# Swapping the rotated query halves by SBUF to SBUF transfers in an attention and FFN kernel

## The reference, cut to what matters

```python
q_nope = (q_c @ W_q_nope).reshape(Bx, Tx, H, NOPE_D)
q_rope = (q_c @ W_q_rope).reshape(Bx, Tx, H, ROPE_D)      # ROPE_D = 64
# rope: x * cos + rotate_half(x) * sin,  rotate_half(x) = concat(-x[32:], x[:32])
q = jnp.concatenate([q_nope, _apply_rope(q_rope, cos, sin)], axis=-1)
attn = softmax(causal(q @ k.T * scale));  out = attn @ v
```

## Time and profile before

| | |
|---|---|
| median of 3 runs | 709.99 us (708.76 to 710.64) |
| span of the profiled execution | 704.9 us |
| difference of the median to that span | 5.1 us |
| busy: TensorE, VectorE, ScalarE, GpSimd | 88%, 76%, 65%, 68% of the span |
| granted TensorE clock, mean | 0.951 |

### The profile page before, as it was taken

How to read it: one execution, slowest core, us unless ns; L and a number is a source line. 1 busy time by engine, 2 the same in 40 slices (tenths; PEclk the granted TensorE clock), 3 DMA queues, 4 the chain that set the end, 5 groups by cost and what they waited for, 6 DMA issues and landing times.

```text
span 704.9 us, 15757 instructions
## 1 busy us (share of the span) xinstructions
PE 622.8 (88%) x6279; PEld 486.1 (69%) x6282; DVE 534.4 (76%) x822; ACT 460.4 (65%) x715; POOL 477.0 (68%) x256
## 2 busy tenths in 40 slices
PE   7989888768989989998998998999899989985956
PEld 5666566557867678776876786778678867774635
DVE  6734889965667968786877777878778777875896
ACT  3465755666766757675768767767687677764754
POOL 2478499955577687768877777877797878710226
PEclk9687999999999999999999999999999999997979
DMA  9773975688898998999989998999799879796003
GB/s 260 255 236 125 225 153 95 109 156 169 206 165 150 159 166 162 147 163 186 181 137 157 156 149 150 165 178 168 131 165 157 151 132 162 134 153 106 9 1 119
DMA packets 323607, 108.32 MB, mean 154 GB/s; under 512 B 305808, under 2 KB 314576, under 8 KB 323408
## 3 DMA queue, kind: packets, MB, share of 16 engines
q1 hardware_dynamic: 322752, 106.74, 79.6%
q10 hardware_dynamic: 784, 0.59, 0.3%
HBM read 21.30 MB, written 10.49 MB: 45 GB/s over the span
## 4 chain that ended last, share of the span: by engine, by line
PE 40%; DVE 27%; ACT 11%; issue 10%; DMA 6%; POOL 5%; SPq 1%; POOLq 0%; DVEq 0%; ACTq 0%
PE psum L1066 37%; DVE small L869 10%; DVE p_src L877 6%; ACT psum L685 5%; DMA pt<-p_src 4%; ACT p_src L679 2%; DMA acc<-in_L_attn_x 2%; DVE o_lo L901 2%; DVE hid L1046 1%; ACT o_hi L667 1%; DVE small L1015 1%; POOL res L540 1%; DVE acc L768 1%; DVE acc L907 1%; PE psum L1267 1%
## 5 line engine op out<-in xcount | busy, mean ns | idle before, releaser
L679 ACT ACTIVATE p_src<-psum,small 128x1024 f16<-128x1024 f32 (+7 forms) x256 | 183.3, 742 | 177.9 <-DVE small L869 177.8
L869 DVE TENSOR_REDUCE small<-psum 128x1 f32<-128x1024 f32 (+7 forms) x256 | 186.3, 748 | 35.0 <-PE psum L1066 34.6
L877 DVE TENSOR_TENSOR p_src<-psum,p_src 128x1024 f16<-128x1024 f32 (+2 forms) x192 | 182.3, 949 | 33.0 <-ACT psum L685 32.5
L685 ACT ACTIVATE psum<-psum,small 128x1024 f32<-128x1024 f32 (+7 forms) x256 | 178.0, 718 | 0.0
L1066 PE MATMUL psum<-k_hi,q_hi 128*128 128x512 f32 (+2 forms) x384 | 159.2, 415 | 20.5 <-DVE p_src L877 10.1
L1066 PE MATMUL psum<-kv_tok,pt 128*128 128x65 f16 (+1 forms) x3456 | 144.3, 197 | 30.6 <-DVE p_src L877 16.7
L1066 PEld LDWEIGHTS psum<-kv_tok,pt 128*128 128x128 f16 x3456 | 121.4, 99 | 71.0 <-issue 35.3
L473 POOL TENSOR_TENSOR q_swap<-q_raw,sin_sb 32x1024 f32<-32x1024 f32 x32 | 75.8, 2370 | 97.7 <-ACT q_raw L613 97.1
L1066 PE MATMUL psum<-k_hi,q_lo 128*128 128x512 f32 (+2 forms) x384 | 133.8, 348 | 0.0
L1066 PE MATMUL psum<-k_lo,q_hi 128*128 128x512 f32 (+2 forms) x384 | 133.3, 347 | 0.0
L1066 PEld LDWEIGHTS psum<-k_hi,q_hi 128*128 128x128 f32 x384 | 75.6, 197 | 29.3 <-issue 12.7
(11 more groups left out here) (160 smaller groups left out, 924.4 us busy)
## 6 DMA issues: line engine op xcount, KB each, us to landing
pt<-p_src SPq DMA_TRANSPOSE x288, 3.5
wq_split<-w_split SPq DMA_DIRECT2D x4, 1024.0 KB, 5.0
k_rotated<-k_split SPq DMA_DIRECT2D x8, 512.0 KB, 3.4
wq<-wq_split SPq DMA_DIRECT2D x16, 256.0 KB, 4.0
acc<-in_L_attn_x SPq DMA_DIRECT2D x4, 512.0 KB, 7.7
ffn_t<-in_L_attn_W_o SPq DMA_DIRECT2D x1, 2048.0 KB, 19.4
k_hi<-k_rotated SPq DMA_DIRECT2D x8, 256.0 KB, 4.4
k_lo<-k_rotated SPq DMA_DIRECT2D x8, 256.0 KB, 4.9
```

The source lines that it names most:

```text
L679: ins = act.activation(p_src[u][:, 0, at:at + w], psum[:, COLS[i]:COLS[i] + w], ACT.Exp, bias=nb)
L685: ins = act.activation(ps, ps, ACT.Exp, bias=nb)
L869: dve.tensor_reduce(sm["mcol"][:, NT * (n % 2) + i:NT * (n % 2) + i + 1], psum[:, COLS[i]:COLS[i] + (i + 1) * P], AX.X, ALU.max, negate=True)\
L877: dve.tensor_tensor(p_src[u][:, 1, :], psum[:, o:o + WIDE[u]], p_src[u][:, 0, :], ALU.subtract)\
```

## The change

Three edits go together. The second GpSimd product goes away: SP copies the two halves of the raw query, swapped, from `q_raw` to `q_swap` by two SBUF to SBUF transfers of 32 partitions and 4 KB each (128 KB per transfer), and POOL multiplies all 64 partitions by the sine table in one instruction and subtracts instead of adding. POOL's wait for the copy of chunk 1 becomes a wait for these transfers, and SP takes over the wait for that copy and one for the previous head's rotation, which frees `q_swap`. SP issues the transfers ahead of the turning of unit 4 (in step 1: of unit 5), those of heads 0 and 1 ahead of the last weight stores of the prologue. And unit 1, which has 512 keys, joins `ONCE`: its two halves go in one turning transfer.

```diff
-ONCE = (3, 4, 5)
+ONCE = (1, 3, 4, 5)
...
+            def swap_halves(m, *chunks):
+                for idx in chunks:
+                    sp.wait_ge(misc_used(idx), USERS_AHEAD[idx] + 1)
+                if m:
+                    sp.wait_ge(S["pool_step"], 3 * m)
+                hr = ROPE // 2
+                for a in range(2):
+                    sp.dma_start(q_swap[a * hr:(a + 1) * hr, :], q_raw[m % 2][(1 - a) * hr:(2 - a) * hr, :])\
+                      .then_inc(S["swap_in"], 16)
...
             for r in range(2):
                 load_wq(r, r)
+            swap_halves(0, 0, 1)
+            swap_halves(1, 2, 3)
             store_wq(2)
             store_wq(3)
...
+                        if n + 2 < LAST and u == (5 if n == 1 else 4):
+                            swap_halves(n + 2, misc_index(n, "query", 0), misc_index(n, "query", 1))
                         turn_unit(n, u)
...
-            def rotate(n, idx):
+            def rotate(n):
                 raw = q_raw[n % 2]
-                pool.wait_ge(misc_used(idx), USERS_AHEAD[idx] + 1)
-                pool.tensor_tensor(q_swap[0:HR, :], raw[HR:ROPE, :], sin_sb[HR:ROPE, :], ALU.mult)\
-                    .then_inc(S["pool_step"], 1)
-                pool.wait_ge(S["pool_step"], 4 * n + 1)
-                pool.tensor_tensor(q_swap[HR:ROPE, :], raw[0:HR, :], sin_sb[0:HR, :], ALU.mult)\
-                    .then_inc(S["pool_step"], 1)
-                pool.wait_ge(S["pool_step"], 4 * n + 2)
+                pool.wait_ge(S["swap_in"], 32 * (n + 1))
+                pool.tensor_tensor(q_swap[:, :], q_swap[:, :], sin_sb[0:ROPE, :], ALU.mult).then_inc(S["pool_step"], 1)
                 pool.tensor_tensor(raw[0:ROPE, :], raw[0:ROPE, :], cos_sb[0:ROPE, :], ALU.mult)\
                     .then_inc(S["pool_step"], 1)
-                pool.wait_ge(S["pool_step"], 4 * n + 3)
-                pool.tensor_tensor(raw[0:ROPE, :], raw[0:ROPE, :], q_swap[:, :], ALU.add).then_inc(S["pool_step"], 1)
-                pool.wait_ge(S["pool_step"], 4 * n + 4)
+                pool.wait_ge(S["pool_step"], 3 * n + 2)
+                pool.tensor_tensor(raw[0:ROPE, :], raw[0:ROPE, :], q_swap[:, :], ALU.subtract).then_inc(S["pool_step"], 1)
+                pool.wait_ge(S["pool_step"], 3 * n + 3)
```

More of the change, by code:

```diff
@@ L256, in build @@
             score_done max_done hi_done exp_done lo_done pv_done rest_done head_read misc_full misc6_used misc7_used
-            pool_step qhi_done qlo_done o_hi_done norm_step
+            swap_in pool_step qhi_done qlo_done o_hi_done norm_step
             att_pool att_sp f_quant_dve
@@ L466, in _ @@
             weight_low(1)
-            HR = ROPE // 2
-            def rotate(n, idx):
+            def rotate(n):
                 raw = q_raw[n % 2]
-                pool.wait_ge(misc_used(idx), USERS_AHEAD[idx] + 1)
-                pool.tensor_tensor(q_swap[0:HR, :], raw[HR:ROPE, :], sin_sb[HR:ROPE, :], ALU.mult)\
-                    .then_inc(S["pool_step"], 1)
-                pool.wait_ge(S["pool_step"], 4 * n + 1)
-                pool.tensor_tensor(q_swap[HR:ROPE, :], raw[0:HR, :], sin_sb[0:HR, :], ALU.mult)\
-                    .then_inc(S["pool_step"], 1)
-                pool.wait_ge(S["pool_step"], 4 * n + 2)
+                pool.wait_ge(S["swap_in"], 32 * (n + 1))
+                pool.tensor_tensor(q_swap[:, :], q_swap[:, :], sin_sb[0:ROPE, :], ALU.mult).then_inc(S["pool_step"], 1)
                 pool.tensor_tensor(raw[0:ROPE, :], raw[0:ROPE, :], cos_sb[0:ROPE, :], ALU.mult)\
                     .then_inc(S["pool_step"], 1)
-                pool.wait_ge(S["pool_step"], 4 * n + 3)
-                pool.tensor_tensor(raw[0:ROPE, :], raw[0:ROPE, :], q_swap[:, :], ALU.add).then_inc(S["pool_step"], 1)
-                pool.wait_ge(S["pool_step"], 4 * n + 4)
+                pool.wait_ge(S["pool_step"], 3 * n + 2)
+                pool.tensor_tensor(raw[0:ROPE, :], raw[0:ROPE, :], q_swap[:, :], ALU.subtract).then_inc(S["pool_step"], 1)
+                pool.wait_ge(S["pool_step"], 3 * n + 3)
             def split_query(n):
@@ L496, in _ @@
             pool.wait_ge(S["wqr_lo"], 2 * 2)
-            rotate(0, 1)
+            rotate(0)
             pool.wait_ge(S["down_psum"], 2 * NPART)
@@ L516, in _ @@
                 if n + 1 < LAST:
-                    rotate(n + 1, misc_index(n - 1, "query", 1) if n else 3)
+                    rotate(n + 1)
                     split_query(n + 1)
```

## The result

| | before | after |
|---|---|---|
| median (lowest to highest) | 709.38 us (704.4 to 710.64, 4 runs) | 724.68 us (721.96 to 731.43, 4 runs) |
| span of the profiled execution | 704.9 us | 720.1 us |
| mean granted TensorE clock | 0.951 | 0.944 |

The change makes the kernel 2.2% slower: ratio 1.0225, 95% interval 1.0155 to 1.0295. In a later comparison of the same two kernels it was 1.0285 (1.0234 to 1.0336), 729.47 us against 711.34. A ratio leaves out every execution that is more than 1.5% above the fastest of its kernel, so it need not be that of the two medians. The forecast was 718.2 us within 706.6 to 728: the sign is right, the measured time is within the range, and 15 us were lost where 8 were forecast. That it lies inside was close: in the later comparison 18 us were lost, and 729.47 is above the range.

What follows compares the result with a forecast made beforehand. Bound: when `q_lo` is ready for a head's first score product, not POOL's work. Terms 6.6 + 3.0 - 3.4 + 2.0 = +8.2 us on the 704.9 span gave 713.1, plus 5.1 to the median: 718.2 us, range 706.6 to 728.

Steps and rivals of the forecast that it cites:

- Together 6.1 us from copy to landing, then 11.0: 17.1 us.: Time from ScalarE's copy of chunk 1 through the swap's landing and POOL's work to `q_lo`: 17.1 us, before 13.5.
- The estimate of 2.3 us: Second copy's landing by the skill page's fixed part plus bytes; basis of the no-change rival, 709.3 us, chance 0.18.
- No transfer has SBUF at both ends.: Claim that the trace before held no such landing, so 3.4 us was taken from the key stores.
- Heads 17, 21, 25, 29 late by 10.4 us.: First score products of these heads, room 14.5 us each, start 2.6 us late each for `q_lo`, 10.4 us in all.
- Part comes back ... That is 3.8 us.: TensorE's idle time in the steps behind late heads 17, 21, 25 and 29 takes back 3.8 us, leaving +6.6.
- 1.8 us after the copy: In SP's list, unit 3's turning issue ends 1.8 us after ScalarE's copy, and the swap's issue follows.
- The heads with n mod 4 = 0 and 2 ... nothing.: These heads have room of 18 us and more before their first product, so they lose nothing.
- Heads 9 and 13, -3.4.: POOL starts these queries late behind a key piece; `q_lo` comes at 247.1, not 248.8, for head 9: -3.4 us for both.
- Unit 5, +2.0.: Unit 5's turning, issued behind the copies, makes TensorE wait 0.5 us in each of four tight steps: +2.0 us.
- covered: Prologue: head 0's swap lands at about 49.6, `q_lo` at 60.6, before first scores at 63.23, with 2.6 us left.
- the rebate: The 3.8 us that TensorE's idle time in steps behind late heads 17, 21, 25 and 29 was to take back.
- heads 11 to 31 in steps of four: Six heads with room of 15.9 to 17.4 us, late by up to 1.2 us each: +3.0 us in all.

Runs made afterwards that it cites:

- swap_only: The changed kernel with unit 1 again in two turning transfers, so the swap alone: 734.89 us, ratio 1.0378 to the kernel before.
- unwaited_copies: The changed kernel with the copies reading the cosine table, POOL not waiting for them and the rotation left out of the result: 704.14 us, ratio 0.9921.
- cosine_first: The changed kernel with POOL doing the cosine product first, into another buffer, while the copies are under way: 704.25 us, ratio 0.995 to the kernel before.
- second profile: The changed kernel run and profiled once more, nothing changed: span 723.7 us, median 729.47 us, ratio 1.0285 to the kernel before.
- fill_stall: The changed kernel with 20 idle TensorE products ahead of the `q_lo` wait in steps 17, 21, 25 and 29: 721.37 us, ratio 1.0167.
- merge_only: The kernel before with only unit 1 put in one turning transfer, no swap: 711.53 us, ratio 0.9972.
- act_issue: The changed kernel with the copies issued on ScalarE's own queue, right behind its copy of chunk 1: 732.14 us, ratio 1.0343 to the kernel before.

## Why the prediction was right, and where it was off

- **"Together 6.1 us from copy to landing, then 11.0: 17.1 us."** Right within 0.7 us: 16.4 to 17.7 in most heads. The sum is better than its parts, which is luck: at head 17 SP was free after 1.30 us, the first issue cost 1.30 and the second copy landed in 3.0, where I had 1.8, 0.9 and 3.4. swap_only, unwaited_copies and cosine_first agree that this chain, and not the load, costs the time. The estimate of 2.3 us worked out from the Trainium skill (DMA: Bandwidth & Descriptors, Anatomy of one DMA), whose fit is for transfers issued by GpSimd, was too low for the copies where they stand, 2.9, but it fits the fastest ones (2.2) and is near the 2.5 of those ahead of unit 3's turning. How busy the engines were for that fit the section does not say.
- **"No transfer has SBUF at both ends."** Wrong: the turnings go from `p_src` to `pt`, both in SBUF, and their landings stand in the trace before, here those of L375:

```profile
DMA to landing us min/median/max: 2.4/3.2/8.6
```

  They would have been nearer rows than the key stores, and their median of 3.2 is close to the 3.4 that was taken.
- **Heads 17, 21, 25, 29 late by 10.4 us.** Measured 9.1, and 9.4 in the second profile. Right.
- **"Part comes back ... That is 3.8 us."** This step failed, in two ways. Nothing came back: +0.7 us, with +2.0 for unit 5 in it that did not occur. The idle time in those steps did go (length and busy time are the same in three of four), but the busy time rose by 1.3 to 1.5 us in three of them, since TensorE, having stood for about 3 us, went on at half its clock. fill_stall, with the clock at 1.00, has 70.8 us in the four steps, 2.9 below the kernel before. And most of that is not late heads being absorbed: merge_only takes 2.0 us out of the same steps with every query on time, since their idle time was mostly waits for `pt`. The rows to see it by were there: I had read of head 9 only that its wait of 2.89 us would shrink, not what the clock did behind that wait. The windows of the kernel before show it:

```profile
245.40:248.80 3.40, 0.57 (x3) 0.13 (x1) 3.37 (x6) 1.97 (x4) 3.32 (x2) 1.00 0.86 234
248.80:252.20 3.40, 3.35 (x30) 2.40 (x31) 1.57 (x2) 0.63 (x1) 1.91 (x2) 0.67 1.31 139
```

- **SP "1.8 us after the copy".** Taken from one step and used for all. It held for heads 17, 21, 25 and 29 (1.3 to 3.0 us) but was 4.8 to 7.5 us for heads 7, 10, 14, 15 and 26, where SP is behind its own list. In step 14 this is most of +3.2 us where I had +0.4; for heads 23 and 27 SP was on time (1.9 and 1.8 us) and the second copy's landing, 3.9 and 3.6 us, was longer than the 3.4. Together these heads cost +6.3 us (+5.1 in the second profile) where I had +3.0.
- **"The heads with n mod 4 = 0 and 2 ... nothing."** Wrong for heads 10 and 14, whose `q_lo` came 21.5 and 20.6 us after the copy; TensorE waited 0.67 and 0.62 us for it. The cost is small, +0.7 us in steps 9 and 13.
- **Heads 9 and 13, -3.4.** Measured -3.8, with 0.7 given up in the steps behind. Right in sum; in the first profile it is 1.4 and 2.4 where 1.7 was forecast for each.
- **Unit 5, +2.0.** Not there: in steps 17, 21, 25 and 29 of after TensorE never waits for `pt`. The copies do lengthen such waits elsewhere, 8.3 us in all against 4.2 in merge_only: 1.8 us of it in steps 9 and 13 and 1.8 in step 31, where nothing was charged.
- **The prologue, "covered".** Nearly: head 0's swap landed at 53.1 and not 49.6, since its landing took 6.8 us behind the weight loads; `q_lo` was done at 63.9 and the first scores started at 64.12, 0.9 us later. "The copies' waits cost SP nothing" did not hold here either: ahead of head 1's pair SP stood 13.5 us for head 0's rotation (the kernel before has 17.4 us of waits for ScalarE at this place). Steps 0 to 7 gave another 1.8 us (3.8 in the second profile), with both signs and with granted clocks that differ both ways; their cause was not looked for by experiment.
- **POOL 75 us less busy.** 77.3. And as forecast it was worth nothing while the swap stood in front of it.

By its terms the forecast was 7.2 us low: about 2.5 from the rebate and unit 5 together, 3.3 from heads 11 to 31 in steps of four, 2.7 from the prologue and the start of the loop, less 1.3 of a lateness put too high; the rests cancel. That half clock behind the waits took the rebate is shown by fill_stall. That SP's lag is due to its list being full is read from the timeline; act_issue, where copies outside this list are issued 0.07 us behind ScalarE's copy and heads 10 and 14 lose their lateness, agrees.

## What to carry to other kernels

When work is taken off an engine and a transfer put in front of the rest, price the chain from the last input to the first user, not the busy time: here 77 us less of POOL's work lost 15 us, and turned into a gain of 0.5% only when a product was moved under the transfer's landing. Before counting on idle time in the next step to take back a wait, look at the granted clock behind an existing wait of that length; where it falls, the wait costs more than its length. And read the queue's lag in the fullest step, not in the one that is easiest to read.

## What the runs showed of the hardware beyond expectation

- TensorE worked at 1.00 up to a wait of 2.94 us (head 17) or 3.64 us (head 25) and in the 3.4 us behind it at 0.50 to 0.52; behind one of 3.71 us in the second profile the whole step was at 0.84. Idle products ahead of the waits kept it at 1.00, worth 8.1 us over the kernel.
- Copies from SBUF to SBUF of 128 KB land in 2.2 us at best. Behind unit 3's turning on the same queue the median was 2.9 us, ahead of it 2.5, and on another engine's queue beside it 5.0: being issued first did not mean landing first. With the pair taken apart, the medians of first and second copy are 3.1 and 2.7 behind the turning, 2.3 and 2.6 ahead of it, 4.1 and 5.8 on ScalarE's queue.
- A POOL product takes 2.38 us with 64 partitions as with 32, so two products of 32 partitions into one of 64 is a real saving of a whole product.
